# Router logits of the down projection: the operand that stands still is exchanged

## What is computed

```python
def _moe_linear(x, router_w, expert_w):        # x: tokens x width
    logits = x @ router_w.T                    # 8 numbers for each token
    vals, idx = jax.lax.top_k(logits, 2)
    probs = jax.nn.softmax(vals, axis=-1)
    ...                                        # combine[token, expert]
    for e in range(n_exp):
        out = out + combine[:, e:e + 1] * (x @ expert_w[e].T)
    return out
...
g = _moe_linear(xt, router_gate, w_gate)       # 128 -> 512
u = _moe_linear(xt, router_up, w_up)           # 128 -> 512
inter = jax.nn.silu(g) * u
d = _moe_linear(inter, router_down, w_down)    # 512 -> 128
```

## Time and profile before

| | before |
|---|---|
| runs | 318.58, 319.29, 320.14 us; median 319.29 |
| span of the profiled execution | 317.6 us |
| TensorE matmul busy | 284.1 us (89%) |
| VectorE busy | 198.8 us (63%) |
| ScalarE busy | 85.8 us (27%) |
| GpSimd busy | 106.1 us (33%) |

### The profile page before, as it was taken

One profiled execution on the slowest core, in us unless ns is written; L12 is line 12 of the kernel. 1 busy time (PEld: TensorE's weight loads), 2 busy tenths in 40 slices (PEclk: granted clock), 3 DMA queues, 4 the chain that ended last, 5 costly groups with the idle time before them and its releaser, 6 DMA issues.

```text
span 317.6 us, 4970 instructions
## 1 busy us (share of the span) xinstructions
PE 284.1 (89%) x1899; PEld 206.0 (65%) x1899; DVE 198.8 (63%) x550; ACT 85.8 (27%) x150; POOL 106.1 (33%) x120
## 2 busy tenths in 40 slices
PE   6549978477987989999999999999999999999992
PEld 2235544244765758787876777777778778788771
DVE  4985573664157667548774963696568748653374
ACT  3603646113221612421141115211411312221010
POOL 4562755542202740640334036003602420410001
PEclk9958976655699999999999999999999999999999
DMA  7932254000000000000000000000000000000000
GB/s 220 343 106 83 75 178 155 0 2 0 1 2 0 3 0 3 0 2 0 2 8 2 1 10 0 0 2 8 3 0 2 8 2 0 11 1 10 0 0 17
DMA packets 5553, 10.03 MB, mean 32 GB/s; under 512 B 917, under 2 KB 3349, under 8 KB 5525
## 3 DMA queue, kind: packets, MB, share of 16 engines
q1 hardware_dynamic: 4666, 8.77, 8.4%
q10 hardware_dynamic: 864, 0.94, 0.9%
HBM read 9.19 MB, written 0.52 MB: 31 GB/s over the span
## 4 chain that ended last, share of the span: by engine, by line
PE 74%; DVE 16%; issue 3%; POOL 2%; ACT 2%; DMA 1%; POOLq 0%; SPq 0%; DVEq 0%
PE PS L893 26%; PE PS L941 13%; PE PS L717 5%; PE PS L869 5%; PE PS L710 4%; PE PS L825 3%; PE PS L802 3%; PE PS L836 3%; PE PS L797 2%; DVE CAND L1024 2%; PE PS L839 2%; PE PS L814 2%; DVE ROOM L1205 2%; PE PS L916 2%; DMA XT<-x_t 1%
## 5 line engine op out<-in xcount | busy, mean ns | idle before, releaser
L893 PE MATMUL PS<-WH,XH 128*128 128x512 f32 x128 | 57.7, 451 | 0.0
L557 POOL TENSOR_TENSOR ROOM<-X,CGU 128x512 f32<-128x512 f32 x32 | 33.2, 1040 | 58.7 <-DVE CGU L1149 38.5
L893 PE MATMUL PS<-WH,XL 128*128 128x512 f32 x128 | 51.2, 400 | 0.0
L893 PE MATMUL PS<-WL,XH 128*128 128x512 f32 x128 | 51.1, 399 | 0.0
L1156 DVE TENSOR_TENSOR XL<-PS,XH 128x512 fp32r<-128x512 f32 x32 | 22.0, 687 | 30.6 <-ACT XH L662 30.4
L662 ACT CAST XH<-PS 128x512 fp32r<-128x512 f32 x32 | 18.8, 586 | 58.7 <-PE PS L869 58.7
L893 PEld LDWEIGHTS PS<-WH,XL 128*128 128x128 f32 x128 | 24.4, 190 | 5.8
L893 PEld LDWEIGHTS PS<-WH,XH 128*128 128x128 f32 x128 | 24.3, 190 | 5.0 <-issue 0.6
L893 PEld LDWEIGHTS PS<-WL,XH 128*128 128x128 f32 x128 | 24.7, 193 | 2.4
L492 POOL TENSOR_SCALAR ZR<-ZMV 128x1 f32<-128x1 f32 x8 | 2.4, 300 | 70.3 <-DVE ZMV L1111 70.3
L540 POOL TENSOR_SCALAR_AFFINE_SELECT PT<-PT 128x1024 f32<-128x1024 f32 x16 | 18.1, 1134 | 22.3 <-ACT PT L645 22.3
(11 more groups left out here) (165 smaller groups left out, 512.7 us busy)
## 6 DMA issues: line engine op xcount, KB each, us to landing
ROOM<-w_gate SPq DMA_DIRECT2D x4, 512.0 KB, 8.4
ROOM<-w_up SPq DMA_DIRECT2D x4, 512.0 KB, 4.0
ROOM<-w_down SPq DMA_DIRECT2D x4, 512.0 KB, 4.6
RO<-rows SPq DMA_DIRECT2D x1, 516.0 KB, 7.8
X<-x_tok ACTq DMA_DIRECT2D x1, 512.0 KB, 3.9
XT<-x_t SPq DMA_DIRECT2D x2, 256.0 KB, 6.2
CT<-ctx_t SPq DMA_DIRECT2D x1, 512.0 KB, 5.8
y_out<-ROOM SPq DMA_DIRECT2D x8, 64.0 KB, 1.5
```

The costliest lines, as they stand in the source:

```text
L557: g.tensor_tensor(XE[:, k % 2, :, :], X[:, t, None, :].broadcast_to([P, 4, P]), CGU[:, t, r, 4 * q:4 * q + 4, None].broadcast_to([P, 4, P] ...
L893: last = mm(PS[:, product_bank(t, r), :], a[:, r, cut], w[:, r, e * I:(e + 1) * I], start=e == 0 and n == 0, stop=e == E - 1 and n == 2)
```

## The change

The operands of L change places. The activations, 128x128 a chunk, are loaded and stand still; the router's columns are streamed, high and low side by side as 16 columns against the high activations, and the 8 high columns against the low activations. The result has tokens on partitions at once, as two sums of 8 numbers, which VectorE adds when it fetches them. The turn and ScalarE's copy ahead of it are gone; the places of the steps in the list stay.

```diff
@@ tiles
-        RDH = sb("RDH", [P, IC * E], F32R)
-        RDL = sb("RDL", [P, IC * E], F32R)
+        RDS = sb("RDS", [P, IC, 2, E], F32R)
...
-        LT = sb("LT", [E, P])
@@ ScalarE
-                elif what == "L":
-                    t, = args
-                    act.wait_ge(f_ld, t + 1)
-                    s.copy(LT[:, :], PS[0:E, LOGIT, 0:P]).then_inc(f_lt, 1)
@@ TensorE
                     high, low = inner(t)
                     for c in range(IC):
-                        for n, (w, a) in enumerate(((RDH, high), (RDL, high), (RDH, low))):
-                            last = mm(PS[0:E, LOGIT, 0:P], w[:, c * E:(c + 1) * E], a[:, c * P:(c + 1) * P],
-                                      start=c == 0 and n == 0, stop=c == IC - 1 and n == 2)
+                        cut = slice(c * P, (c + 1) * P)
+                        mm(PS[:, LOGIT, 0:2 * E], high[:, cut], RDS[:, c, :, :].rearrange("p a e -> p (a e)"),
+                           start=c == 0, stop=False, skip_group_check=True)
+                        last = mm(PS[:, LOGIT, 0:E], low[:, cut], RDS[:, c, 0, :],
+                                  start=False, stop=c == IC - 1, skip_group_check=True)
                     last.then_inc(f_ld, 1)
-                elif what == "LL":
-                    t, = args
-                    pe.wait_ge(f_lt, t + 1)
-                    transpose(PS[:, LOGIT, P:P + E], LT[:, :], ID[0:E, 0:E]).then_inc(f_ll, 1)
@@ VectorE
                 elif what == "RD":
                     dve.wait_ge(ld_t, NLT)
-                    v.tensor_copy(RDH[:, :], RD[:, :]).then_inc(c_dve, 1)
+                    v.tensor_copy(RDS[:, :, 0, :], RD[:, :].rearrange("p (c e) -> p c e", e=E)).then_inc(c_dve, 1)
                     dve.wait_ge(c_dve, 3)
-                    v.tensor_tensor(RDL[:, :], RD[:, :], RDH[:, :].bitcast(F32), ALU.subtract).then_inc(c_dve, 1)
+                    v.tensor_tensor(RDS[:, :, 1, :], RD[:, :].rearrange("p (c e) -> p c e", e=E),
+                                    RDS[:, :, 0, :].bitcast(F32), ALU.subtract).then_inc(c_dve, 1)
...
                 elif what == "LL":
-                    dve.wait_ge(f_ll, t + 1)
-                    v.tensor_copy(DLG[:, :], PS[:, LOGIT, P:P + E]).then_inc(f_lg, 1)
+                    dve.wait_ge(f_ld, t + 1)
+                    v.tensor_reduce(DLG[:, :], PS[:, LOGIT, 0:2 * E].rearrange("p (a e) -> p e a", a=2), AX_X, ALU.add)\
+                        .then_inc(f_lg, 1)
                     dve.wait_ge(f_lg, t + 1)
```

More of the change, by code:

```diff
@@ L327, in decoder_layer @@
         f_ld = sem("f_ld")
-        f_ll = sem("f_ll")
         f_d0 = sem("f_d0")
@@ L342, in decoder_layer @@
         f_ith = sem("f_ith")
-        f_lt = sem("f_lt")
         f_de = sem("f_de")
```

## The result

The changed kernel takes 317.28 us in the median of its runs, the kernel before, on the same chips, 319.15: a ratio of 0.9946, 95% interval 0.9919 to 0.9972, or 0.54% faster. The forecast was 317.5 and 0.56%.

The account below looks back on a forecast made before the run. TensorE was taken to bound most of the chain (74%), VectorE 16%. Turn -2.04, L +0.33, tail -0.11 and reduction +0.02 sum to -1.80 us: 317.5 us forecast, range 316.2 to 318.9.

Parts of the forecast that it names:

- L: Logits step among the expert matmuls: eight pairs of 0.11 us, 0.88 in all, 0.11 longer than its 0.77.
- The turn: Turn of the logits between expert matmuls: holds TensorE 0.34 us; removing it gains that in tiles 1 to 5 and 7.
- loads in the open: Rival, chance 0.08: loads cannot run behind such short matmuls, pairs take 0.25 us, kernel 5.2 us slower, 324.5.
- The rule against it: Skill page's rule that loads overlap only across differing row groups; each pair's load would stand open. Prediction held rows contradict it.
- Tiles 2 to 4: Turn of the row maxima there waits for VectorE; 0.11 of that 0.15 us wait absorbs L's extra time.
- Tile 6: VectorE leads from 261.79 to 277.67 us, so TensorE's saving of 0.34 - 0.11 there only lengthens its wait.
- The tail: After the last tile, VectorE no longer waits for the turn to land: 0.11 us gained, bounds 0 and 0.2.
- The reduction: VectorE's copy becomes a reduction of 16 numbers to 8: 0.01 us more, seen in tile 6 and the tail, 0.02.
- other engines take the gain: Rival, chance 0.16: VectorE leads throughout tiles 2 to 4, whose gain goes into the next wait; only -0.8 us, 318.5.
- more is gained: Rival, chance 0.08: tile 6 also keeps the turn's 0.34 and L's 0.11 is absorbed everywhere; -2.5 us, 316.8.

Follow-up runs that it names:

- e3_wide: The changed kernel with the 16 router columns streamed eight times over, 128 columns in place of 16; ratio to the kernel before 0.9927.

## Why the prediction was right, point by point

From tile 1 on the kernel gained 1.8 us, and 1.80 was forecast. That the median, too, came within 0.3 us of its forecast is in part luck, since the start of the kernel alone moves by 2.4.

- *The turn.* Right, 0.35 against 0.34, with its cause: the same cost came back from a turn that waits for nobody, and fell to 0.11 when the turn used all rows. What the prediction lacked is the reason: the load doesn't begin early because the turn has fewer rows.
- *L.* Right in kind, 0.13 longer and not 0.11. The 0.90 is 0.03 from the first matmul to the second, 0.78 for the seven spacings from 155.77 to 156.55, 0.111 each, and 0.09 to the expert's stream; the prediction had 8 x 0.11. The loads set the pace (e3_wide). The rival of loads in the open would have had pairs 0.25 us apart.
- *The rule against it.* The Trainium skill, "TensorE: Matmul & The Clock Gate", "Part 3: Packing small matmuls — row/col tiling", has loads overlap only where the row group differs. These traces show otherwise: loads on the same 128 rows ran under the matmuls, the first of each train wholly (0.03 us from the first matmul to the second), and it is behind a change to 8 or 32 rows that TensorE stood.
- *Tiles 2 to 4, and what absorbs L there.* Right: moving L behind A gave it all back as a wait for VectorE, and from the first gate expert of tile 2 to that of tile 5 the changed kernel gained 1.05 us, three times LL's 0.35.
- *Tile 6.* The sum came out by luck, the step was wrong. I wrote that VectorE leads from 261.79 to 277.67, so that whatever TensorE saves there only lengthens the wait. But the run with the turn of 128 rows lost its 0.10 us in tile 6 as elsewhere, and the run with the router still kept its 0.26. What stands in its place: turn 28 on TensorE releases GpSimd's product, and the small VectorE instruction that it falls on lasts until the product ends. The profile counts this as VectorE's own work, and so the chain there read as VectorE's: two DC take 1.17 us together in the rows below and 0.48 in the tail. The kernel before, at the same place (GpSimd, then VectorE):

```profile
275.33 1.04 POOL L557 TENSOR_TENSOR ROOM<-X,CGU 128x512 f32<-128x512 f32 x1 [1.91 <-PE PS L869]
...
275.42 1.17 DVE L1192 TENSOR_SCALAR DC<-RO,DIF,DP 128x8 f32<-128x8 f32 x2
...
276.83 0.69 DVE L1156 TENSOR_TENSOR XL<-PS,XH 128x512 fp32r<-128x512 f32 x1
```

  There the product fell on the first of the two DC, and its end (275.33 + 1.04 = 276.37) left 276.83 - 276.37 = 0.46 us of VectorE's work to XL; with the turn LL gone the product starts earlier against VectorE's chain, falls on the instruction ahead of DC, and leaves 275.27 - 274.49 = 0.78. The 0.32 lost there cancels LL's gain of 0.35, and with L's 0.13 on top tile 6 became some 0.1 us longer, near the forecast of no change. The product was held back in the changed kernel alone; for the kernel before the account rests on these rows and on the run with the turn of 8 rows, which brought the product back onto DC and the 0.31 with it.
- *The tail.* 0.20 against 0.11, the upper bound given: I had counted only the pause after VectorE's last accumulation, but the reduction, which no longer waits, starts at 304.67, before the accumulation ahead of it ends at 303.25 + 1.51 = 304.76.
- *The reduction* cost nothing (0.16 us against the copy's 0.17); 0.02 was allowed for.

The rival that other engines take the gain fell: it would have had LL's gain in tiles 2 to 4 lost to VectorE, and there it stayed. The rival that more is gained fell with tile 6, which kept nothing.

## What to carry to other kernels

Exchanging the operands of a small product doesn't pay by the columns it no longer streams: behind loads of 128 columns in 32 bits a matmul of up to 128 columns cost its load here, 0.11 us. Here it paid because it made a turn on 8 rows needless. Keeping the router still, with its columns side by side, and turning at full height took another 0.7 us off: the cheap loads stay and the switch of rows goes. Where a chain seems to run on one engine, look at what another engine does at the same time, and hold it back, before believing it. And compare stretches of the trace, not medians, where the start of the kernel wanders by more than the effect.

## What the runs showed of the hardware

- A matmul on 8 or 32 rows behind one on 128 starts 0.32 us after it where one on 128 rows starts after 0.23, and a single turn between experts costs 0.35 us on 8 rows against 0.11 on 128.
- A VectorE instruction on one number a partition, 0.16 us alone, took 0.92 us under a GpSimd product of 1.04 us. From tile 1 on the eleven profiles have 64 such cases, a DP or the first DC under a product, and each ends 0.01 to 0.03 us after it. The Trainium skill, "SBUF — State Buffer", section "SBUF: two separate sides", says that GpSimd and a VectorE instruction with two inputs in SBUF share a port pair that one of them holds for its whole instruction; the trace agrees, with 274.51 against 274.49 for the ends.
- The start of tile 1 lay between 115.1 and 117.5 us in profiles of kernels that do nearly the same up to there, and it goes with the mean granted clock of that stretch, 0.79 to 0.85. What makes the clock differ was not tried.
